# Attention of the third layer: the softmax shift added by VectorE instead of TensorE, and the head sums scaled on ScalarE and added on GpSimd

## The reference, cut to what matters

```
Q = (x @ Wq.T).reshape(b, n, H, R)          # H = 8, R = 64
K = (x @ Wk.T).reshape(b, n, H, R)
V = (x @ Wv.T).reshape(b, n, H, d)          # d = 128
attn = jnp.einsum('bnhr,bmhr->bhnm', Q, K)
attn = jax.nn.softmax(attn, axis=-1)
out = jnp.einsum('bhnm,bmhd->bnd', attn, V)
```

## Time and profile before

| | |
|---|---|
| time, median of 3 | 1781.58 us (1781.22 to 1786.49) |
| the profiled execution | 1781.18 us, of which the span is 1779.1 us |
| busy of the span | PE 95%, DVE 56%, ACT 47%, POOL 23% |
| third layer | from about 643 us to 1453 us of the span |
| the loop over head pairs, second batch | pair 0 from 809 us, `times_v` of pair 3 ends at 853.7 us |

### The profile page before, as it was taken

One profiled execution on the slowest core, in us unless ns is written; L12 is line 12 of the kernel. 1 busy time (PEld: TensorE's weight loads), 2 busy tenths in 40 slices (PEclk: granted clock), 3 DMA queues, 4 the chain that ended last, 5 costly groups with the idle time before them and its releaser, 6 DMA issues. The chain is left out here.

```text
span 1779.1 us, 22932 instructions
## 1 busy us (share of the span) xinstructions
PE 1695.2 (95%) x8670; PEld 1011.7 (57%) x8670; DVE 995.9 (56%) x1661; ACT 836.3 (47%) x1041; POOL 403.0 (23%) x325
## 2 busy tenths in 40 slices
PE   7899999997999989999999999999999997999996
PEld 4232222223555656877878787877778762444443
DVE  4555555544665444454555454454555447888885
ACT  4767777775435443343334343343334333444442
POOL 1000000000663222030211212030211205655552
PEclk8699999998889989999999999999999998999998
DMA  2222222223008610000000000000000010000001
GB/s 78 51 48 48 48 48 49 48 48 125 1 6 192 160 25 1 1 1 2 0 2 1 1 1 1 1 1 1 1 1 1 1 59 1 1 1 1 1 0 48
DMA packets 19257, 49.16 MB, mean 28 GB/s; under 512 B 912, under 2 KB 1808, under 8 KB 18256
## 3 DMA queue, kind: packets, MB, share of 16 engines
q1 hardware_dynamic: 19152, 47.73, 11.4%
HBM read 45.23 MB, written 2.36 MB: 27 GB/s over the span
## 5 line engine op out<-in xcount | busy, mean ns | idle before, releaser
L498 ACT ACTIVATE probs<-ps_ring 128x1024 f32<-128x1024 f32 x256 | 245.9, 1023 | 87.5 <-PE ps_ring L735 84.5
L1822 PEld LDWEIGHTS ps_o<-v,probs 128*128 128x128 f32 x2048 | 235.3, 192 | 31.1 <-issue 25.3
L1822 PE MATMUL ps_o<-v,probs 128*128 128x129 f32 x2048 | 248.1, 278 | 1.8 <-ACT probs L1547 1.2
L1547 ACT ACTIVATE probs<-ps_ring 128x1024 f32<-128x1024 f32 x128 | 127.0, 1024 | 212.4 <-PE ps_ring L1803 212.3
L1628 DVE TENSOR_REDUCE negmax<-ps_o 128x2 f32<-128x1024 f32 x64 | 78.5, 1226 | 137.1 <-PE ps_o L1778 137.1
L749 PE MATMUL ps_o<-probs,v 128*32 128x512 f32 x1024 | 139.3, 618 | 0.7 <-DVE o_sb L559 0.6
L1540 ACT ACTIVATE xn<-ps_ring,pack 128x512 f32<-128x512 f32 x64 | 40.6, 685 | 162.7 <-PE ps_ring L1387 162.7
L2002 POOL TENSOR_TENSOR rs<-r,state 128x512 f32<-128x512 f32 x64 | 86.2, 1348 | 115.0 <-DVE state L2149 114.8
L1641 DVE RECIPROCAL rden<-ps_o 128x2 f32<-128x2 f32 x128 | 21.4, 167 | 144.4 <-PE ps_o L1822 144.4
L735 PEld LDWEIGHTS ps_ring<-q_stack,k_stack 32*128 32x128 f32 x512 | 32.0, 186 | 123.4 <-issue 101.0
L2149 DVE TENSOR_TENSOR_SCAN state<-decay,state,kv 128x511 f32<-128x511 f32 x64 | 91.9, 1436 | 6.9 <-issue 1.6
(11 more groups left out here) (389 smaller groups left out, 3464.2 us busy)
## 6 DMA issues: line engine op xcount, KB each, us to landing
cwb<-combine_by_expert SPq DMA_DIRECT2D x8, 2048.0 KB
score<-score_by_expert SPq DMA_DIRECT2D x15, 1024.0 KB, 7.8
pack<-pack_dram SPq DMA_DIRECT2D x1, 3840.0 KB, 15.1
pack<-pack_dram SPq DMA_DIRECT2D x1, 2507.0 KB, 8.8
x<-x_in SPq DMA_DIRECT2D x2, 1024.0 KB, 6.0
out<-x SPq DMA_DIRECT2D x1, 2048.0 KB, 6.3
pack<-pack_dram SPq DMA_DIRECT2D x1, 1479.0 KB, 6.4
pack<-pack_dram SPq DMA_DIRECT2D x1, 1140.0 KB, 9.3
```

The lines of the kernel that those rows point to most:

```text
L498: nc.scalar.activation(probs[n % 3][:, 2 * half:2 * half + 2, :], ps, ACT.Exp, scale=float(HD0) ** -0.5).then_inc(read, 1)
L1547: nc.scalar.activation(probs[:, n % 2, m, :, :], ps, ACT.Exp).then_inc(read, 1)
L1822: last = nc.tensor.matmul(ps_o[:, i, k * (D + 1):(k + 1) * (D + 1)], probs[:, (b * PAIRS + p) % 2, m, j, queries], v[:, m, h, :], start=(m ...
```

## The change

For pairs 1 to 3, PE no longer adds the row to each of the four score blocks. A new ring use ("shift", b, p) comes before the pair's first score block: one pair of matmuls `ones_row` times `sh_row` alone. ACT copies it to `spread` in SBUF (`spread_shift`, 128 x 1024), DVE adds it to each score block from PSUM and writes `probs` (`add_shift`, 128 x 1024), and ACT takes the exponential in place in `probs`. `times_v` of such a pair waits for the four exponentials. Pair 0 stays as it was. `sh_row` is one buffer instead of two; the second transfer of a pair waits until the shift before was made.

`normalise` is cut to the reciprocal. ACT scales each step's two blocks of 128 x 128 (`scale_head`), for head 0 into `att`, for others into `o_scaled`; POOL adds these to `att` (`add_head`, 128 x 256). The final transposes wait for POOL. The subtraction that makes `xl` of the next batch moves in POOL's list behind the additions of head 4. `ones_row` is made on the chip by POOL's memsets instead of being loaded.

```
             for s in range(HALVES):
                 if p + 1 < PAIRS and s < 3:
+                    if s == 0:
+                        order.append(("shift", b, p + 1))
                     order.append(("score", b, p + 1, s))
...
+            def add_head(b, h, i):
+                if h:
+                    pool.wait_ge(o_read, (b * H2 + h) * 2 + i + 1)
+                    both = att[:, 2 * i:2 * i + 2, :]
+                    nc.gpsimd.tensor_tensor(both, both, o_scaled[:, i, :, :], ALU.add).then_inc(att_added, 1)
+                    if i:
+                        pool.drain()
...
             def exponent(b, p, m):
                 n = b * PAIRS + p
+                weight = probs[:, n % 2, m, :, :]
+                if p:
+                    was_read(act, ("score", b, p, m))
+                    nc.scalar.activation(weight, weight, ACT.Exp).then_inc(probs_ready, 1)
+                    return
...
+            def spread_shift(b, p):
+                ps, read = filled(act, ("shift", b, p))
+                nc.scalar.activation(spread[:, :, :], ps, ACT.Copy).then_inc(read, 1)
+
+            def scale_head(b, h, i):
+                n = (b * H2 + h) * 2 + i
+                act.wait_ge(rden_ready, n + 1)
+                if h > 1:
+                    act.wait_ge(att_added, (b * (H2 - 1) + h - 2) * 2 + i + 1)
+                for k in range(2):
+                    to = o_scaled[:, i, k, :] if h else att[:, 2 * i + k, :]
+                    last = nc.scalar.activation(to, ps_o[:, i, k * (D + 1):k * (D + 1) + D], ACT.Copy, scale=rden[:, i, k:k + 1])
+                last.then_inc(o_read, 1)
...
                 for p in range(PAIRS):
                     for s in range(HALVES):
+                        if p + 1 < PAIRS and s == 0:
+                            spread_shift(b, p + 1)
+                        scale_head(b, 2 * p + s // 2, s % 2)
                         if p + 1 < PAIRS and s < 3:
                             exponent(b, p + 1, s)
...
-                nc.vector.reciprocal(rden[:, i, :], o[:, :, D])
-                dve.drain()
-                for k in range(2):
-                    m = 2 * i + k
-                    if h == 0:
-                        last = nc.vector.tensor_scalar(att[:, m, :], o[:, k, 0:D], rden[:, i, k:k + 1], None, ALU.mult)
-                    else:
-                        last = nc.vector.scalar_tensor_tensor(att[:, m, :], o[:, k, 0:D], rden[:, i, k:k + 1], att[:, m, :],
-                                                              ALU.mult, ALU.add)
-                last.then_inc(o_read, 1)
+                if n >= 2:
+                    dve.wait_ge(o_read, n - 1)
+                nc.vector.reciprocal(rden[:, i, :], o[:, :, D]).then_inc(rden_ready, 1)
+
+            def add_shift(b, p, m):
+                n = b * PAIRS + p
+                if n >= 2:
+                    dve.wait_ge(o_done, (n - 1) * HALVES)
+                was_read(dve, ("shift", b, p))
+                ps, read = filled(dve, ("score", b, p, m))
+                nc.vector.tensor_tensor(probs[:, n % 2, m, :, :], ps, spread[:, :, :], ALU.add).then_inc(read, 1)
...
                         normalise(b, 2 * p + s // 2, s % 2)
+                        if p + 1 < PAIRS and s < 3:
+                            add_shift(b, p + 1, s)
+                            if s == 2:
+                                add_shift(b, p + 1, 3)
                         if p + 2 < PAIRS and s < 2:
                             maximum(b, p + 2, 2 * s)
                             maximum(b, p + 2, 2 * s + 1)
...
-                for j in range(2):
-                    last = nc.tensor.matmul(ps[:, j, :], single(ones_row[head_rows(j), :]), single(sh_row[n % 2][head_rows(j), :]),
-                                            start=False, stop=True)
+                if p == 0:
+                    last = add_row(ps, False)
...
-                    if p == 0:
+                    if p:
+                        pe.wait_ge(probs_ready, (b * (PAIRS - 1) + p) * NBLK)
+                    else:
...
                         if p + 1 < PAIRS and s < 3:
+                            if s == 0:
+                                shift(b, p + 1)
                             scores(b, p + 1, s)
```

More of the change, by code:

```diff
@@ L62, in constants @@
     i = np.arange(P)
-    ones_row = np.zeros((P, P), np.float32)
-    ones_row[[0, 64]] = 1
     same8 = (i[:, None] // 8 == i[None, :] // 8).astype(np.float32)
     c = {"ident": np.eye(P, dtype=np.float32), "mean_all": np.full((P, P), 1 / D, np.float32),
-         "mean_head": same8 / 8, "sum_head": same8, "ones_row": ones_row}
+         "mean_head": same8 / 8, "sum_head": same8}
     place = np.zeros((P, 2, 32), np.float32)
@@ L134, in packed @@
     third_whole = {
-        "ones_row2": k["ones_row"],
         "s1_2": f["L2_ffn_w1_s"].reshape(FT, P).T, "s2_2": f["L2_ffn_w2_s"].reshape(FT, P).T,
@@ L1416, in layer2_mix @@
         rows = sb("shift_rows2", [2 * NBLK, 2, P])
-        sh_row = [sb(f"shift_row2_{i}", [P, T]) for i in range(2)]
+        sh_row = sb("shift_row2", [P, T])
+        spread = sb("spread_shift2", [P, 2, T])
+        o_scaled = sh["xn"][:, at(3)].rearrange("p (i k d) -> p i k d", i=2, d=D)
         rden = sb("rden2", [P, 2, 2])
@@ L1424, in layer2_mix @@
         ring_read = [sem(f"ring2_read{i}") for i in range(RING2)]
-        ones_ready, scales_ready, v_ones = sem("ones_ready2"), sem("scales_ready2"), sem("v_ones2")
+        constants_ready = sem("constants_ready2")
+        ONES_ROW, SCALES = 1, 2
         rows_zero = sem("rows_zero2")
@@ L1480, in _ @@
                 was_read(sp, ("turn", n // PAIRS, n % PAIRS))
-                if n >= 2:
-                    filled(sp, ("score", (n - 2) // PAIRS, (n - 2) % PAIRS, NBLK - 1))
+                if n:
+                    b, p = divmod(n - 1, PAIRS)
+                    filled(sp, ("shift", b, p) if p else ("score", b, p, NBLK - 1))
                 for j in range(2):
-                    sp.dma_start(sh_row[n % 2][64 * j:64 * j + 1, :].rearrange("o (m t) -> o m t", t=P),
+                    sp.dma_start(sh_row[64 * j:64 * j + 1, :].rearrange("o (m t) -> o m t", t=P),
                                  rows[NBLK * j:NBLK * j + NBLK, n % 2, :]).then_inc(sh_loaded[n % 2], 16)
@@ L1488, in _, with low_x @@
         def _(pool):
[L1489 to L1492, removed]
+            nc.gpsimd.memset(att[:, 0, :], 0.0)
+            nc.gpsimd.memset(sh_row[:, :], 0.0)
+            pool.drain()
+            for j in range(2):
+                nc.gpsimd.memset(att[64 * j:64 * j + 1, 0, :], 1.0).then_inc(rows_zero, 1)
+                pool.drain()
+            nc.gpsimd.memset(v[:, :, :, D:D + 1], 1.0).then_inc(rows_zero, 1)
+            def low_x(b):
                 pool.wait_ge(xh_ready, b + 1)
                 nc.gpsimd.tensor_tensor(single(xl[:, :]), xb[:, :], xh[:, :], ALU.subtract).then_inc(xl_ready, 1)
+            def add_head(b, h, i):
[4 more added lines that the diff above has]
+                    if i:
+                        pool.drain()
+            low_x(0)
+            for b in range(B):
                 for t in range(FT):
@@ L1503, in _ @@
                                                 ).then_inc(hid_low_ready, 1)
+                for h in range(H2):
+                    for i in range(2):
+                        add_head(b, h, i)
+                    if h == 4 and b + 1 < B:
+                        low_x(b + 1)
         @block.scalar
@@ L1546, in exponent @@
                 ps, read = filled(act, ("score", b, p, m))
-                nc.scalar.activation(probs[:, n % 2, m, :, :], ps, ACT.Exp).then_inc(read, 1)
+                nc.scalar.activation(weight, ps, ACT.Exp).then_inc(read, 1)
+            def spread_shift(b, p):
[10 more added lines that the diff above has]
+                last.then_inc(o_read, 1)
             nc.scalar.preload_act_table_set("natural_log_exp_and_others")
@@ L1551, in _ @@
             rstd(0)
-            act.wait_ge(scales_ready, 1)
+            act.wait_ge(constants_ready, SCALES)
             for b in range(B):
@@ L1660, in _ @@
             nc.vector.tensor_scalar(half_s1[:, :], w["s1_2"], 0.5, None, ALU.mult)
-            nc.vector.tensor_copy(single(ones_row[:, :]), w["ones_row2"]).then_inc(ones_ready, 1)
+            dve.wait_ge(rows_zero, 2)
+            nc.vector.tensor_copy(single(ones_row[:, :]), att[:, 0, :]).then_inc(constants_ready, 1)
             dve.drain()
-            nc.vector.tensor_tensor(s12[:, :], half_s1[:, :], w["s2_2"], ALU.mult).then_inc(scales_ready, 1)
+            nc.vector.tensor_tensor(s12[:, :], half_s1[:, :], w["s2_2"], ALU.mult).then_inc(constants_ready, 1)
             centre(0)
@@ L1790, in turn_max, with add_row, shift @@
                                     ident).then_inc(done, 1)
+            def add_row(ps, start):
+                for j in range(2):
+                    last = nc.tensor.matmul(ps[:, j, :], single(ones_row[head_rows(j), :]), single(sh_row[head_rows(j), :]),
```

(24 more changed lines are left out.)

1 line of the change is left out of this document (added).

## The result

The changed kernel takes 1807.33 us (median of 4, 1806.84 to 1807.91) against 1783.32 us of the kernel before in the same comparison: ratio 1.0133, 95% interval 1.0115 to 1.0152. It is 24 us slower. The forecast was 1804 us, 22.9 us slower, in a range of 1788 to 1815. The profiled execution took 1806.84 us with a span of 1804.6 us. The third layer, from its first matmul to the next layer's first load, went from 643.02:1454.26 (811.2 us) to 645.57:1482.72 (837.2 us), 25.9 us more. The layers around it differ by 2.5 us one way and 3.0 us the other, in code that the change doesn't touch; they cancel to within half a us.

A forecast was written before the change was run, and what follows sets the result against it. The prediction took the pair loop as PE-bound without a gap. Pair loops cost 18.7 us net of PE's saving, plus 2.8, 1.0 and 0.4 elsewhere: 22.9 us over 1781, so 1804 us, range 1788 to 1815.

The forecast's parts named there:

- The saving: PE's row matmuls in pairs 1 to 3: four dropped, one gained, 0.69 us a pair, 16.6 us over 8 batches.
- Pair 0, plus 1.28: Pair 0's loop: DVE's list delays the last exponential, PE stands about 1.1 us; 12.92 becomes 14.20 us a batch.
- the signs that the prediction itself named for being wrong: Adds shorter than 1.1 us, PE idle elsewhere (ended by SP or by DVE's maxima), or a clock under 1.00.
- The tail's size: After a pair's last scores: add 1.22 plus in-place exponential 0.97 us plus handovers, covered by 1.84; pair 2 plus 0.43.
- Pair 1, plus 0.54: Pair 1's loop, where the next batch's variance waits for add 2 and step 3 hides the exponential: 14.13 becomes 14.67 us.
- The ends: Outside the pair loops: batch heads 2.8 us in all, the layer's last output 1.0, the start 0.4.
- late table load: At a batch's end ACT's table load follows the last scaling: tanh 0.75 us late, costing PE some 0.4, 7 times.
- The sum: Pair loops 18.7 us, plus 2.8, 1.0 and 0.4 at heads, end and start: 22.9 us slower.
- Faster: Rival for the pair loops: DVE's work is hidden and PE keeps its 16.6 us, giving 1766 us; chance 0.05.
- "tail only" rival: Rival for the pair loops: DVE never late through maxima, only the tail counts; 1786 us, no measurable change; chance 0.08.
- The late row: Rival: bounds for SP's shift-row transfers and the table load come on top, giving 1812 us; chance 0.10.
- The clock: Rival: stalls in the pair loops make PE run a tenth of the time at 1.2 GHz, 1820 us; chance 0.10.

The follow-up runs named there:

- e7: Kernel before, but DVE adds the shift for pair 3 only, whose scores come two blocks each in steps 0 and 1: 1772.07 us, ratio 0.9957.
- e8: e7 with one line different, so all rows are TensorE's and only the order of pair 3's scores differs from before: 1779.09 us, ratio 0.9991.
- e3: Changed kernel, with the maxima of pairs 2 and 3 taken over the first 64 of 512 keys: 1804.48 us, ratio 1.013.
- e5: Kernel before, with head sums scaled on ACT and added on POOL, except each batch's last head pair, normalised on DVE: 1779.87 us, ratio 1.0007.
- e1: Changed kernel with the normalisation given back to DVE; shift, adds and in-place exponentials kept: 1832.97 us, ratio 1.0291.
- e6: Changed kernel with pair 3's scores made two blocks in step 0 and two in step 1 of pair 2: 1792.9 us, ratio 1.0077.

## Why the prediction was right, point by point

**The saving.** 0.23 us for a pair of row matmuls, 0.69 a pair: e7 against e8 shows 0.67. Right.

**Pair 0, plus 1.28.** Measured plus 1.44. The chain as written was DVE's list, from the copy of the shift to the fourth add. It does run without a pause, and the adds stand where it puts them: the third starts 8.71 us after the shift (8.76 forecast). But the statement that DVE "is now the longer list" and so sets pair 0 did not hold: with the maxima nearly gone (e3) the pair shortened by 0.23 us only. What counts is the tail behind the last scores, add and exponential of block 3, with add 2 ahead of them, which the prediction used for pair 2 alone. That the number came out all the same is luck: both chains reach the third add at the same time. The ring waits were never counted for pair 0, and a wait on DVE's maxima, small as it is (0.24 us), was one of the signs that the prediction itself named for being wrong.

**The tail's size.** Up to the end of the exponential the forecast is within 0.1 us (12.16 us after the shift where 12.18 was forecast in pair 0, 10.54 where 10.46 was in pair 2). The exponential in place takes 1.057 us, not 0.97: the rows compared a tanh from PSUM with an exponential from SBUF at 512 elements, two functions. From PSUM the same function takes 1.023. This hardly moved the sum, since the handover from the last add was 0.03 us where 0.10 was taken. What was missing is the last step: from the exponential's end at 827.50 to PE's first matmul are 0.25 us, not 0.05. Pair 2 was forecast at 10.51 and measured at 10.79. The Trainium skill's table (VectorE: DVE Perf Modes, section on the TRN2 errata) has the SBUF source 0.04 us dearer by an estimate from its cycles, the trace 0.034: here the page was right and the reading of the rows wrong.

**Pair 1, plus 0.54.** Measured plus 0.50. Its variance waits for add 2 and covers the exponential, as worked out: it starts 839.71 - 829.70 = 10.01 us after the shift, forecast 10.04:

```profile
839.71 1.12 PE L1764 MATMUL ps_ring<-xn,pack 128*128 128x512 f32 x2 [0.53 <-DVE probs L1698]
```

**The ends.** The head of a batch lost 0.46 us where 0.4 was counted for the late table load; the layer's end 0.77 where 1.0 was; the start 0.4 as counted (first matmul of the gates 9.38 us after the layer's first matmul, 8.95 before). In e5, which removes the first two, nothing measurable is left of them. POOL's 256 elements take 0.73 us, under the 0.85 taken, and cost nothing in the loop.

**The sum.** 8 x 1.44 + 7 x 0.50 + 1.44 + 8 x 0.71 + 7 x 0.46 + 0.77 + 0.43 = 26.6, where pair 1 of the last batch is taken as a pair 0; the layer itself shows 25.9 and the time 24.

**The rivals.** Faster did not come, for the reason given, but the cure that e7 shows was not seen: not a cheaper add, but scores that end earlier and a pair without maxima. The "tail only" rival, 1786 us, had the right mechanism and the wrong price: it left out the ring waits (0.35 and 0.24 us in pairs 0 and 1, and of the variance's 0.53 in pair 1 all but 0.19), 16 x 0.59 + 7 x 0.34 = 12 of the 21 us between it and what was measured; the rest is a tail taken too short and the table load. The late row never appeared: no wait of PE in the layer's pair loops was ended by a transfer. The clock did fall, in e1, not in the change.

Not tried: a version in which pairs 1 and 2 gain as well. The copy's ring wait and DVE's four maxima stand against it, and no run here has shown a way past them.

## What to carry to other kernels

Work taken off a saturated engine is a gain only if the chain that replaces it fits under what that engine does meanwhile. Before moving work, count what follows the last result of a stage: here one instruction of 1.02 us under a cover of 1.84 became two of together 2.3, and the 0.69 us saved turned into 0.5 to 1.4 us lost; in the pair where the last results were issued one step earlier, the cover came back. When two chains end within 0.2 us of each other, a profile can't tell which one counts: shorten one (e3) and reorder the other (e6).

## What the runs showed of the hardware

Stalls of TensorE of 1.16 us, in pairs 0 and 2 of a batch, left the clock at 1.00 (the changed kernel). In e1, five of nine stalls of 2.16 us or more were followed by a fall to about half, four were not (one of them of 2.52 us), and one fall followed a wait of 1.53 us; each fall cost about 1.7 us. VectorE's add of PSUM and SBUF at 128 x 1024 lasts 1.23 us, but the next instruction starts 1.14 us after it. An exponential of 128 x 1024 takes 1.057 us in place in SBUF and 1.023 from PSUM. In the changed kernel ScalarE starts 0.03 us after the VectorE instruction that it waits for (818.22 to 818.25), VectorE 0.09 after ScalarE (816.90 to 816.99), and TensorE's first matmul 0.25 after ScalarE (827.50 to 827.75).
